# Context normalisation of batches 2 to 7: ScalarE in place of VectorE

## The reference

```
x1 = x + attn(ada_ln(x), ada_ln(ctx)) @ Wp + bp            # layer 0: cross attention
x2 = x1 + gate * (self_attn(ln(x1) * (1 + s) + t) @ Wo)    # layer 1: self attention
x3 = x2 + attn(ln(x2) * g + b, ctx) @ Wc                   # layer 2: cross attention, context not normalised
y  = x3 + gate * mlp(ln(x3) * (1 + s) + t)                 # MLP with 1024 hidden units
```

## Time and profile before

| | |
|---|---|
| median of 3 runs | 476.73 us (476.11 to 478.85) |
| profiled execution | 477.31 us, of which the span is 475.2 us |
| TensorE (PE) busy | 429.6 us, 90% of the span |
| VectorE (DVE) busy | 287.1 us, 60% |
| ScalarE (ACT) busy | 238.0 us, 50% |
| GpSimd (POOL) busy | 179.5 us, 38% |
| mean granted TensorE clock | 0.982 of full speed |
| context normalisation on VectorE, all 8 batches (L1112) | 24 instructions, 10.7 us |

### The profile page before, as it was taken

How to read it: one execution, slowest core, us unless ns; L and a number is a source line. 1 busy time by engine, 2 the same in 40 slices (tenths; PEclk the granted TensorE clock), 3 DMA queues, 4 the chain that set the end, 5 groups by cost and what they waited for, 6 DMA issues and landing times. The chain is left out here.

```text
span 475.2 us, 11732 instructions
## 1 busy us (share of the span) xinstructions
PE 429.6 (90%) x4464; PEld 326.8 (69%) x4464; DVE 287.1 (60%) x748; ACT 238.0 (50%) x517; POOL 179.5 (38%) x284
## 2 busy tenths in 40 slices
PE   5887879998989899798997999999999899899996
PEld 5765557666667586476775677776677577688894
DVE  2658576767766667367567675678676597332112
ACT  1233254655645465445654656657666566752230
POOL 6264336345527216315532527431414512340000
PEclk9998899999999999889998999999999999999999
DMA  8568773418433634471351163652264240000000
GB/s 211 128 155 186 210 180 105 110 35 185 135 92 111 177 100 130 112 188 51 104 138 42 54 157 93 156 145 49 59 153 98 62 101 2 2 1 11 19 21 29
DMA packets 50399, 48.67 MB, mean 102 GB/s; under 512 B 14584, under 2 KB 47312, under 8 KB 50344
## 3 DMA queue, kind: packets, MB, share of 16 engines
q1 hardware_dynamic: 40988, 37.78, 32.0%
q10 hardware_dynamic: 9356, 10.14, 7.4%
HBM read 17.27 MB, written 0.93 MB: 38 GB/s over the span
## 5 line engine op out<-in xcount | busy, mean ns | idle before, releaser
L1140 DVE TENSOR_REDUCE nmax<-bank 112x1 f32<-112x375 f32 x256 | 132.3, 541 | 67.2 <-PE bank L647 65.6
L877 ACT ACTIVATE prob<-bank 125x448 f32<-125x448 f32 (+1 forms) x224 | 119.8, 544 | 98.2 <-PE bank L620 96.8
L647 PE MATMUL bank<-k_stack,q_stack 96*128 96x375 bf16 (+1 forms) x256 | 80.2, 335 | 12.9 <-DVE nmax L1140 5.3
L620 PE MATMUL bank<-q_stack,k_stack 99*128 99x112 bf16 x768 | 67.8, 213 | 3.0 <-DMA q_stack<-nm_t 1.9
L620 PEld LDWEIGHTS bank<-q_stack,k_stack 99*128 99x128 bf16 x768 | 51.8, 98 | 23.8 <-issue 5.5
L726 PE MATMUL bank<-wkv,ctx_t 128*125 128x256 f32 x192 | 52.4, 397 | 0.0
L721 PE MATMUL bank<-ctx_t,wkv 128*128 128x375 f32 x128 | 49.5, 512 | 1.9 <-ACT ctx_t L898 1.9
L673 PE MATMUL bank<-prob,v_tokens 125*17 125x112 f32 x1536 | 50.0, 263 | 0.1
L647 PEld LDWEIGHTS bank<-k_stack,q_stack 96*128 96x128 bf16 (+1 forms) x256 | 25.7, 103 | 31.8 <-issue 13.3
L1376 POOL CAST k_parts<-k_rest 128x375 bf16<-128x375 f32 x32 | 17.5, 546 | 71.5 <-DVE k_rest L1190 71.4
L673 PEld LDWEIGHTS bank<-prob,v_tokens 125*17 125x17 f32 x1536 | 33.3, 98 | 13.5 <-issue 9.8
(11 more groups left out here) (117 smaller groups left out, 723.6 us busy)
## 6 DMA issues: line engine op xcount, KB each, us to landing
k_stack<-k_parts SPq DMA_DIRECT2D x90, 187.5 KB, 3.7
q_stack<-job_part SPq DMA_DIRECT2D x66, 112.0 KB, 2.3
ctx_tokens<-in_ctx_dram ACTq DMA_DIRECT2D x14, 375.0 KB
k_self_stack<-job_part SPq DMA_DIRECT2D x24, 112.0 KB, 2.3
late_space<-in_L_xcond_mlp_w_dram ACTq DMA_DIRECT2D x2, 1024.0 KB, 6.2
late_space<-in_L_xcond_ada_w_dram SPq DMA_DIRECT2D x1, 1536.0 KB, 6.7
gate_self<-gate_rows SPq DMA_DIRECT2D x8, 112.0 KB, 3.7
k_self_stack<-gate_rows SPq DMA_DIRECT2D x1, 896.0 KB, 7.5
```

What stands on the lines that cost most here:

```text
L620: last = pe.matmul(sh.score_t[n % 2][:, j * T:(j + 1) * T], keys, sh.q_all[:, b // 2, o:o + T], start=True, stop=True)
L647: last = pe.matmul(bank[0:m, 0:L], sh.q_all[0:DEEP, b // 2, o:o + m], sh.k_st[CIDX[i] % KRING][0:DEEP, place(k) * L:(place(k) + 1) * L], s ...
L877: act.activation(sh.prob[n % NPROB][0:rows, :], sh.score_t[n % 2][0:rows, 0:GH * T], ACT.Exp, scale=SCALE).then_inc(sg.exp_done, 1)
L1140: dve.tensor_reduce(sh.nmax[i % NMAX][:, place(k):place(k) + 1], bank_of(sh, (i, k))[0:T, 0:L], AX_X, ALU.max, negate=True).then_inc(free_ ...
```

## The change

For batches 2 to 7, ScalarE normalises the context in place of VectorE, at the same step number. ScalarE computes `scale * in + bias`, so GpSimd makes a new small tensor `ctx_shift` = -mean * rstd in two more instructions behind `context_rstd`, with a new semaphore `cst_shift`. Batches 0 and 1 stay on VectorE. The planner's tables are untouched, so no other instruction changes its place.

```diff
+    sh.ctx_shift = sb("ctx_shift", [KT, 2, NT])
+    sg.cst_shift = sems.new("cst_shift")
...
 def scalar_program(act, sh, sg, ins):
+    def norm_context(ci):
+        act.wait_ge(sg.cst_shift, 2 * (ci - 1))
+        for t in range(NT):
+            act.activation(sh.ctx[ci % 2][:, t, :], sh.ctx[ci % 2][:, t, :], ACT.Identity, bias=sh.ctx_shift[:, ci % 2, t:t + 1],
+                           scale=sh.ctx_rstd[:, ci % 2, t:t + 1]).then_inc(sg.xnc_done, 1)
...
         for i, k in TAILS.get(g, []):
             if k == 1:
                 read_ot(i)
+        for ci in XNCS.get(g, []):
+            if ci >= 2:
+                norm_context(ci)
...
 def vector_program(dve, sh, sg):
         for ci, t in STATS.get(g, []):
             if ci >= 2:
                 context_stats(ci, t)
-        for ci in XNCS.get(g, []):
-            if ci >= 2:
-                norm_context(ci)
...
     def context_rstd(ci):
         pool.tensor_tensor(sh.ctx_rstd[:, ci % 2, :], sh.ctx_veps[:, :], sh.half[0:KT, 0:NT], ALU.pow).then_inc(sg.cst_rstd, 1)
+        if ci >= 2:
+            pool.wait_ge(sg.cst_rstd, ci + 1)
+            pool.tensor_tensor(sh.ctx_shift[:, ci % 2, :], sh.ctx_mv[:, ci % 2, :, 0], sh.ctx_rstd[:, ci % 2, :], ALU.mult).then_inc(sg.cst_shift, 1)
+            pool.wait_ge(sg.cst_shift, 2 * (ci - 2) + 1)
+            pool.tensor_scalar(sh.ctx_shift[:, ci % 2, :], sh.ctx_shift[:, ci % 2, :], -1.0, None, ALU.mult).then_inc(sg.cst_shift, 1)
```

## The result

The changed kernel takes 486.35 us (median of 4 runs, 485.5 to 489.36) beside 477.14 us of the kernel before in the same session (476.11 to 478.85): a ratio of 1.0218, interval 1.0172 to 1.0264. It is 9.2 us slower; 483.7 was forecast, from 478.0 to 488.5. The profiled execution took 485.5 us, its span 483.7, at a mean granted clock of 0.974 (0.982 before).

The account below looks back on a forecast made before the run. TensorE, busy 90% of the span, was taken to bound the kernel. Delays of 4.45 us plus clock falls of 1.7 and 0.85 made +7.0 us, taking the median from 476.73 to 483.7 us, range 478.0 to 488.5.

Parts of the forecast that it names:

- Sign and mechanism: Batches 3 to 7: slower, as ScalarE waits in order for the shift, holding up exponentials and X reads TensorE needs.
- The stands: ScalarE idle before its first normalisation of batches 3 to 7: about 4.7, 2.2, 4.1, 2.1 and 1.7 us.
- The prices: One ScalarE normalisation of 256 elements takes 0.56 us; the shift is ready about 0.65 us after the reciprocal deviation.
- The hold of 1.4 us: Three normalisations on ScalarE: what follows starts 1.4 us after the first begins, bounds 1.1 and 1.7.
- Place by place: TensorE's delay at each batch: +1.65, +1.5, +0.5 and +0.8 us at batches 3 to 6, 0 at 2 and 7.
- Batch 2: Step 5: deviation long ready, next key part late by 0.6 us; cost taken at 0, bounds 0 and 0.6.
- the DMA wait at 166 us: Batch 7's delay of +0.45 us goes into TensorE's 1.59 us wait for a maximum's DMA, leaving 0.
- The sum of +4.45: TensorE's delays at batches 3 to 6 added up, +4.45 us, bounds 3.3 to 5.6, before the clock.
- One fall and a half: Clock falls behind TensorE's new waits: one at batch 3 (+1.7 us), one more half covered (+0.85); ends none and four.
- The case of four falls: Rival: the clock falls at all four places, 4.45 + 6.8 = 11.3 us, giving 488.0; chance 0.15.
- VectorE's relief: Rival: shift there whenever ScalarE comes by, so TensorE's waits for VectorE go, 5.2 us faster, 471.5; chance 0.12.
- The rival that only the price counts: Nothing waits and ScalarE bounds these steps: 18 exchanged instructions cost 1.1 us, giving 477.8; chance 0.04.

Follow-up runs that it names:

- late2: The change with ScalarE's normalisation two steps later, one step ahead of the transposes: 478.17 us, ratio 1.0008 to the kernel before.
- late1: The change with ScalarE's normalisation one step later, behind the next exponential and, at batches 3, 4 and 6, the X read: 478.29 us, ratio 1.0001.
- early: The change with the context statistics of batches 3 to 7 three steps earlier, ScalarE's normalisation left in place: 477.61 us, ratio 0.999 to the kernel before.
- early_dve: The kernel before (VectorE normalises) with the context statistics of batches 3 to 7 three steps earlier: 477.09 us, ratio 0.9989.
- early_fill: The kernel early with small matmuls put on TensorE for its remaining waits and ahead of the first self attention: 483.9 us, ratio 1.0089.
- only57: The change for batches 5 and 7 alone, VectorE normalising the others: 481.43 us, ratio 1.0111 to the kernel before.

## Why the prediction was right, and what was off

- **Sign and mechanism: right.** ScalarE stands for the shift, and TensorE's waits for maxima give way to waits for `x_t` at batches 3, 4 and 6 and for `prob` at 5 and 7, as named. The stands were forecast at 4.7, 2.2, 4.1, 2.1 and 1.7 us; the rows show 4.83, 2.33, 4.18, 2.03 and 2.08. That the stand in this place, with the work and the held-up reads behind it, is the cause is shown by late2, which does the same work without a stand, and by late1, whose stands (7.6 us) come behind the `X` read: both take the time of the kernel before.
- **The prices: right.** One normalisation was put at 0.56 us and takes 0.591. The Trainium skill, ScalarE: Activation LUTs, "What ACT_TABLE_LOAD costs", gave an estimate of 0.585, and the trace agrees with it. The hold of 1.4 us was 1.49 (65.61 to 67.10). The shift's two instructions take 0.195 and 0.260 us, 0.65 with their gaps was forecast.
- **Place by place:** +1.65, 1.5, 0.5, 0.8 at batches 3 to 6 were forecast and +1.55, 1.65, 0.55, 1.15 measured. Batch 2 at nothing, right. Batch 7's +0.85 went into the DMA wait at 166 us, as forecast, and it took 0.7 more. The sum of +4.45 stands beside 4.2 by the shifts, 4.4 and 5.0 by the executions. So close an agreement is luck in part: without the 0.7 that the DMA wait took beyond batch 7's share the shifts would say 4.9, and the longer VectorE chain behind batch 6, +0.9, stood nowhere in the forecast.
- **The clock: the term that was too small.** One fall and a half, 2.55 us, was taken. The profiled execution had falls behind three of the new waits (2.65, 1.4 and 1.1 us, together 5.15) and one fewer later, 1.55; the executions together say some 4. The price of 1.7 us for a fall was near; the number of falls was too low. The step that failed is the rule by which falls were counted: batch 4's and 6's idle times of 2.4 and 2.1 us brought falls, batch 5's of 2.24 did not, so the length of one wait doesn't tell. The case of four falls, 488.0, lay 1.7 above the result, the forecast 2.7 below; the truth is between them.
- **The rivals.** VectorE's relief did not reach the places: the shift came 2 to 5 us late at each. Had the context come earlier, the gain would have been small all the same: early was expected at 470 to 475.5 and took 477.61. The rival that only the price counts falls by its number: it gave 477.8 and the change took 486.35. Its price of 1.1 us itself is not excluded, since the intervals of late1 and late2, where it is paid, reach 2 us. The Trainium skill's rule for it (ScalarE: Activation LUTs, "Rules for kernel authors": plain adds and multiplies belong to VectorE) gives the right choice for this kernel, but no run here shows a loss by the price itself.
- **A side row:** VectorE's busy time fell by 6.7 us, not 9. Its context group fell by 8.6 (10.7 to 2.1), while `x_norm` grew from 17.5 to 18.2 and the last step of the chains from 4.6 to 5.3; the latter is the one long instruction at 147.43. And the 0.74 us at batch 4, which the forecast names beside the waits for maxima, is a wait for `x_norm`; its sum does not hang on that.

No version was found that beats the kernel before beyond what can be measured; early_dve, 0.9989 (0.996 to 1.0019), comes nearest.

## What to carry to other kernels

Before work goes to an engine that is idle half of the time, look at when that engine reaches the place and what stands behind it: an in-order engine that runs ahead pays with its wait, and what it holds up (here a read that frees a bank) sets the price, not the busy time. The place in the program matters more than the engine: two steps later, the same work cost nothing that could be measured. And a gain or a loss on the engine that bounds the kernel has to be followed to the next transfer and the next clock fall, either of which can take it back.

## What the runs showed of the hardware that was not expected

- Clock falls vary from execution to execution of one program: the 46 executions of the kernel before had mean clocks of 0.969 to 0.993, and the span goes with them by 0.31 us per us at half clock.
- Of two waits of nearly the same length, one (2.40 us, batch 4) was followed by a fall and the other (2.24 us, batch 5) by none.
- Two waits of TensorE that the profile puts down to "issue" ended 0.1 us after the landing of the keys that the block reads: 71.04 and 71.13 us in early_fill, 237.53 and 237.62 in only57.
- The last part of one set of self keys landed 2.3 us after its issue in the kernel before and 5.8 to 6.7 us after it in six other kernels.
- One 112x16 operation on VectorE (the last step of a maxima chain) took 0.89 us in the change and 0.18 before.
